# Channel attention: 12 of 49 tap tiles of exponentials summed by accumulating DMAs from GpSimd's queue, the total added by TensorE late in the tile

## The chip, the cores and the metric

The kernel runs on one core of one Trainium2 chip. The metric is the device time of one execution, in microseconds (us). PE is TensorE, DVE is VectorE, ACT is ScalarE, POOL is GpSimd, SP is SyncE.

## The reference, cut to what matters

Four layers run one after the other on an image tensor x of 4 x 256 x 64 x 64 float32: a windowed attention, a linear attention with grouped convolutions, a per-channel attention over 7 x 7 neighbours, and a dynamic 3 x 3 convolution. The change lies in the third alone:

```python
q = einsum('bchw,oc->bohw', x, w_q)
kmap = einsum('bchw,oc->bohw', x_pad, w_k)
vmap = einsum('bchw,oc->bohw', x_pad, w_v)
kwin = _unfold2d(kmap, 7)   # + rel_h on the first half of the channels, + rel_w on the other
attn = softmax(q[..., None] * kwin, axis=-1)     # over the 49 taps
out = sum(attn * vwin, axis=-1)
```

So each channel and pixel has 49 exponentials (taps), whose sum divides the sum of exponential times value.

## The kernel before, in words

`channel_attention` (from L1395) puts 128 channels on the partitions. A band is 16 image rows; 4 images make 16 bands (NB). A band has 4 tiles (TPB): 2 halves of the channels, and for each 2 tiles of 8 image rows, 512 pixels (TPX). In all that is 64 tiles of 49 taps. The taps of a tile are worked off in 7 rows of 7 taps ("row o" below is taps 7o to 7o+6). All engines have their order written out by hand: `all_bands(step)` calls a step for each tap of each tile on PE, ACT and DVE, and POOL loops over groups of 4 and 3 taps.

One step j does this:

- DVE (`multiply`, L1998) writes (key + relative bias) x query into one of 3 PSUM banks (`stage`, NST = 3). It waits until ACT has read the tap that used this bank before, so DVE is at most 3 taps ahead of ACT.
- PE (`step`, L1723) adds up the weighted values of tap j-12 (`sum_weighted`, V_LAG = 12), subtracts the upper bound from tap j (`shift`, L1679), and adds up the exponentials of tap j-2 (`sum_exponential`, E_LAG = 2). Both sums are 4 matmuls of 128x128 against an identity (`add_up`, L1686), which turn the tile and accumulate it in `pe_sum` or `pv_sum`.
- ACT (`exponential`, L1847) takes the exponential of tap j out of PSUM into a row buffer `se` (4 buffers of one row, NSE = 4). Before it writes into a buffer again it waits until PE has summed and POOL has weighted what was there. After tap 1 it copies the finished sum of the tile before into `es` (`take_e_sums`, L1835). After tap 46 it places the query of the next tile in PSUM (`place_query`, L1828).
- POOL (`weigh`, L1909) multiplies 4 or 3 taps of exponentials with the values into one of 4 buffers `ev`. PE reads them at step j+12.

Other work is placed at fixed steps. PE projects the next band's keys, queries and values (`project`, L1668): in the first tile of a half at steps 0, 7, 14, 24 and 29, in the second at 2, 6 and 12, each of two matmuls at two steps. DVE inverts the sum of the tile before in four pieces after steps 3, 5, 7 and 9 (`invert`, L2006), divides at step 12 (L2014), and makes the pairs and extremes of the next half's keys: `near_step_of` (L1946, L1950, L1958) at steps 11 to 30 of the first tile, after ACT's copy of the projection (L1821); `extreme_step` (L1974 to L1983) from step 34 of the first tile to step 46 of the second. ACT scales the next band at step 30 of the band's second tile (`normalise`, L1770).

Waits between the engines count on semaphores in units of taps, groups and tiles (`tiles(n, t, per, more)`).

Of the kernel before, what the change touches and what calls it, by code (L numbers as in the profile page):

```python
# [6 lines left out]
ACT = mybir.ActivationFunctionType  # L7
# [6 lines left out]
PART = 128  # L14
# [1368 lines left out]
K2 = 7  # L1383
# [11 lines left out]
def channel_attention(nc, sems, x_in, coef, x_out, stats, w_t, rel, ident_in, zeros):  # L1395
# [3 lines left out]
    with ctx:  # L1399
# [17 lines left out]
        top = [sb(f"top{u}", [PART, BPX], F32R) for u in range(2)]  # L1417
        se = [sb(f"se{i}", [PART, K2, TPX]) for i in range(NSE)]
        ev = [sb(f"ev{i}", [PART, ROW_PARTS[0][1], TPX]) for i in range(NEV)]
        es = sb("es", [PART, TPX])  # L1420
# [28 lines left out]
        exp_done = sem("exp_done")  # L1449
        weighted = sem("weighted")  # L1450
        e_summed = sem("e_summed")
        v_summed = sem("v_summed")
# [14 lines left out]
        ROWS_OF = {"0": (PAD, PAD), "1": (FRESH, RT), "2": (FRESH + RT, RT)}  # L1467
        E_LAG, V_LAG = 2, 12
        Q_AT = NTAP - NST
        INVERT_AT = (3, 5, 7, 9)  # L1470
# [20 lines left out]
        def tiles(n, t, per, more):  # L1491

            return n * (TPB * per) + (t * per + more)
# [65 lines left out]
        def before(t, j, lag):  # L1559

            back = t * NTAP + j - lag
            return back // NTAP, back % NTAP

        def bank_of(t, j):

            g = t * NTAP + j
            return 1 if g == TPB * NTAP - 1 else g % NST

        def bank_lag(t, j):

            return 2 if t * NTAP + j in (1, TPB * NTAP - 1) else NST

        def group_of(j):
            o, i = divmod(j, K2)
            return o * len(ROW_PARTS) + (i >= ROW_PARTS[1][0])
# [67 lines left out]
        def _(pe):  # L1643
# [38 lines left out]

            def add_up(acc, src, j):

                for c in range(NBLK2):
                    last = nc.tensor.matmul(acc[:, c * PART:(c + 1) * PART], lhsT=src[:, c * PART:(c + 1) * PART],  # L1686
                                            rhs=ident[:], is_transpose=True, start=j == 0 and c == 0,
                                            stop=j == NTAP - 1, skip_group_check=True)
                return last

            def sum_exponential(n, t, j, first=False):
                o, i = divmod(j, K2)
                if j == 0 and (t or not first):

                    pe.wait_ge(e_taken, tiles(n, t, 1, 0))
                pe.wait_ge(exp_done, tiles(n, t, NTAP, j + 1))
                add_up(pe_sum, se[(t * K2 + o) % NSE][:, i], j).then_inc(e_summed, 1)

            def sum_weighted(n, t, j, first=False):
                g = group_of(j)  # L1700
                i = j % K2 - ROW_PARTS[g % 2][0]
                if j == 0 and (t or not first):

                    pe.wait_ge(divided, tiles(n, t, 1, 0))
                if i == 0:
                    pe.wait_ge(weighted, tiles(n, t, NG2, g + 1))
                add_up(pv_sum, ev[(t * NG2 + g) % NEV][:, i], j).then_inc(v_summed, 1)

# [14 lines left out]
            def step(n, t, j, first=False, final=False):  # L1723
# [4 lines left out]
                shift(n, t, j)  # L1728
                if t * NTAP + j >= E_LAG or not first:
                    sum_exponential(n, *before(t, j, E_LAG), first=first)  # L1730
                if late:
                    sum_weighted(n, t, 0, first=first)
# [29 lines left out]
        def _(act):  # L1762
# [67 lines left out]
            def take_e_sums(n, t):  # L1830
                act.wait_ge(e_summed, tiles(n, t, NTAP, NTAP))
                if t > 0 or n:

                    act.wait_ge(inverted, tiles(n, t, NINV, 0))
                nc.scalar.activation(es[:], pe_sum[:], ACT.Copy).then_inc(e_taken, 1)  # L1835

            def exponential(n, t, j, first=False):
                o, i = divmod(j, K2)
                g = group_of(j)
                start, size = ROW_PARTS[g % 2]  # L1840
                if i == start and (t * NTAP + j >= NSE * K2 or not first):

                    t0, j0 = before(t, j, NSE * K2)
                    act.wait_ge(e_summed, tiles(n, t0, NTAP, j0 + size))
                    act.wait_ge(weighted, tiles(n, t0, NG2, group_of(j0) + 1))
                act.wait_ge(shifted, tiles(n, t, NTAP, j + 1))
                nc.scalar.activation(se[(t * K2 + o) % NSE][:, i], stage[:, bank_of(t, j), :], ACT.Exp)\  # L1847
                    .then_inc(exp_done, 1)

# [45 lines left out]
        def _(pool):  # L1895
            def weigh(n, t, g, first=False):
# [7 lines left out]
                if t * NG2 + g >= NEV or not first:  # L1904
# [4 lines left out]
                nc.gpsimd.tensor_tensor(split(ev[(t * NG2 + g) % NEV][:, 0:size]),  # L1909
                                        split(se[(t * K2 + o) % NSE][:, i:i + size]),  # L1910
                                        window(v[h], h, u, o, i, size), ALU.mult).then_inc(weighted, 1)

            for x in (xb, *k, *v, near, pair):
                nc.gpsimd.memset(x[:], 0.0).then_inc(cleared, 1)
            for n in range(NB):
                for t in range(TPB):
                    for g in range(NG2):
                        weigh(n, t, g, first=n == 0)

# [655 lines left out]
```

## Time and profile before

| what | us |
|---|---|
| three runs | 7983.3, 7987.79, 7996.58 |
| median | 7987.79 |
| the profiled execution's own time | 7993.27 |
| its span, first to last instruction | 7991.6 |
| channel attention, first to last multiply of DVE | 3314 to 7303 |

The profile is of one execution. Its own time is 5.5 us above the median of the runs. Matmuls are pipelined, and the profile models their ends: the mean of one says less than the distance from one start to the next. Where an engine's busy time fills a stretch, it had no wait there; what is missing is idle time. The two tiles whose rows are read below, called A and B, are the third and the fourth of one band: A (4940.74 to 5003.74 us) is the first tile of a half and has the near steps and the K and Q projections, B (5003.74 to 5063.33 us) is the second and has the V projections. A stretch runs from the start of DVE's multiply of tap 7o to that of tap 7o+7.

### The profile page before, as it was taken

Reading aid. Unit: us, or ns where it says so; the run is one execution under the profiler, and the core shown is the slowest. Engines: PE = TensorE matmul, PEld = TensorE weight load, DVE = VectorE, ACT = ScalarE, POOL = GpSimd, SP = SyncE. Lnnn points to the kernel's source line nnn. Section 1 sums busy time; section 2 is a strip of 40 time slices with the busy share of each in tenths; the row PEclk is TensorE's granted clock in tenths of the full one; section 3 lists DMA queues with packets and bytes.
Section 4 is the critical chain, followed back from the end, with each engine's and each line's share of the span. In section 5 each row is a group of like instructions: output and inputs, shape, how many; then the busy total and the mean of one; then the engine's idle time right before and its main releaser. Section 6 shows DMA issues by size and latency. Waiting matters only on the chain. (4 is left out here: it accounts for less than half of the span.)

```text
span 7991.6 us, 141890 instructions
## 1 busy us (share of the span) xinstructions
PE 7529.3 (94%) x55106; PEld 6489.6 (81%) x55106; DVE 5666.6 (71%) x8853; ACT 3670.7 (46%) x7040; POOL 4566.2 (57%) x2002
## 2 busy tenths in 40 slices
PE   5999998989998999599999999999999999997999
PEld 4777776879997776388888888888888888886999
DVE  5666665334443555688888888888888888896664
ACT  3655655423332332255555555555555555554222
POOL 3555552023332000388888888888888788886232
PEclk9999998999999999799999999999999999998999
DMA  3111113865557873100000000000000000002452
GB/s 142 61 58 67 60 58 122 282 161 144 144 147 194 234 210 109 29 20 23 27 18 17 20 23 27 18 18 19 24 27 18 17 20 24 27 9 93 138 164 78
DMA packets 633018, 617.21 MB, mean 77 GB/s; under 512 B 465525, under 2 KB 498421, under 8 KB 627174
## 3 DMA queue, kind: packets, MB, share of 16 engines
q1 hardware_dynamic: 581318, 483.44, 21.8%
q0 software_dynamic: 33856, 96.69, 3.3%
q10 hardware_dynamic: 17376, 30.54, 1.0%
q8 instruction: 330, 5.41, 0.3%
q14 instruction: 138, 1.13, 0.0%
HBM read 397.01 MB, written 193.76 MB: 74 GB/s over the span
## 5 line engine op out<-in xcount | busy, mean ns | idle before, releaser
L1909 POOL TENSOR_TENSOR e_ev<-e_se,e_v 128x2048 f32<-128x2048 f32 (+1 forms) x896 | 3307.7, 3712 | 760.6 <-ACT e_se L1847 758.1
L1847 ACT ACTIVATE e_se<-e_stage 128x512 f32<-128x512 f32 x3136 | 1867.8, 597 | 1851.4 <-PE e_stage L1679 1792.9
L1998 DVE SCALAR_TENSOR_TENSOR e_stage<-e_k,e_rl,e_qp 128x512 f32<-128x512 f32 x3136 | 2290.5, 747 | 340.7 <-ACT e_se L1847 285.7
L1686 PE MATMUL e_pe_sum<-e_ident,e_se 128*128 128x128 f32 x12544 | 1880.6, 272 | 16.5 <-ACT e_se L1847 12.3
L1686 PE MATMUL e_pv_sum<-e_ident,e_ev 128*128 128x128 f32 x12544 | 1875.4, 273 | 0.5 <-POOL e_ev L1909 0.5
L1686 PEld LDWEIGHTS e_pe_sum<-e_ident,e_se 128*128 128x128 f32 x12544 | 1550.6, 140 | 259.1 <-ACT e_es L1835 21.8
L1686 PEld LDWEIGHTS e_pv_sum<-e_ident,e_ev 128*128 128x128 f32 x12544 | 1477.2, 140 | 204.6 <-issue 203.2
L1679 PE MATMUL e_stage<-e_top,e_minus 128*128 128x512 f32 x3136 | 1507.8, 481 | 89.2 <-DVE e_stage L1998 85.6
L911 POOL DMA_DIRECT2D agg<-c_ot x384 | 334.6, 874 | 878.7 <-ACT c_ot L989 769.1
L403 POOL TENSOR_TENSOR a_pr<-a_pr,a_rden 128x480 f32<-128x480 f32 x512 | 494.1, 985 | 547.6 <-DVE a_rden L636 547.6
L1679 PEld LDWEIGHTS e_stage<-e_top,e_minus 128*128 128x128 f32 x3136 | 595.5, 190 | 143.6 <-DVE e_stage L1998 99.7
L596 ACT ACTIVATE a_pr<-a_ps,a_nmax 128x240 f32<-128x240 f32 x1024 | 459.3, 460 | 386.7 <-DVE a_nmax L630 386.7
L1974 DVE SCALAR_TENSOR_TENSOR e_ext<-e_near,e_rl,e_ext 128x512 f32<-128x512 f32 x768 | 575.3, 749 | 12.1 <-ACT e_ext L1857 11.4
L948 PE MATMUL c_pa<-c_x_high,c_w_high 128*128 128x448 f32 (+1 forms) x1440 | 522.6, 363 | 33.4 <-DVE c_w_low L1014 33.4
L948 PE MATMUL c_pa<-c_x_low,c_w_high 128*128 128x448 f32 (+1 forms) x1440 | 522.2, 363 | 0.0
L948 PE MATMUL c_pa<-c_x_high,c_w_low 128*128 128x448 f32 (+1 forms) x1440 | 522.0, 363 | 0.0
L630 DVE TENSOR_REDUCE a_nmax<-a_ps 128x2 f32<-128x480 f32 x512 | 312.9, 653 | 292.1 <-PE a_ps L484 285.0
L2294 PE MATMUL f_pc<-f_x_high,f_w_high 128*128 128x256 f32 x1536 | 440.3, 287 | 15.2 <-DVE f_xr L2474 13.0
L1958 DVE TENSOR_REDUCE e_near<-e_pair 128x192 f32<-128x768 f32 (+1 forms) x392 | 438.3, 1118 | 0.5
L2251 POOL TENSOR_TENSOR f_x_low<-f_xt,f_x_high 128x2560 fp32r<-128x2560 f32 x32 | 186.1, 5817 | 439.9 <-ACT f_x_high L2328 408.0
L2294 PE MATMUL f_pc<-f_x_low,f_w_high 128*128 128x256 f32 x1536 | 434.7, 283 | 0.0
L2294 PE MATMUL f_pc<-f_x_high,f_w_low 128*128 128x256 f32 x1536 | 434.1, 283 | 0.0
(175 smaller groups left out, 11567.5 us busy)
## 6 DMA issues: line engine op xcount, KB each, us to landing
qkv<-b_ot SPq DMA_DIRECT2D x120, 512.0 KB, 5.9
c_xt<-qkv SPq DMA_DIRECT2D x384, 160.0 KB, 3.8
agg<-c_ot POOLq DMA_DIRECT2D x384, 160.0 KB, 2.5
f_ws<-in_L_w_sets SPq DMA_DIRECT2D x32, 1152.0 KB, 7.9
a_xb<-in_x SPq DMA_DIRECT2D x24, 768.0 KB, 5.1
a_xr<-in_x SPq DMA_DIRECT2D x32, 512.0 KB, 3.8
x<-a_xr SPq DMA_DIRECT2D x32, 512.0 KB, 2.7
b_xc<-x SPq DMA_DIRECT2D x32, 512.0 KB, 5.8
```

The source lines that it names most:

```text
L403: nc.gpsimd.tensor_tensor(w, w, by, ALU.mult).then_inc(normalised, 1)
L596: last = nc.scalar.activation(pr[P % BUF][:, i, e, :], ps[:, 2 * s + i, e * NK:(e + 1) * NK], ACT.Exp, bias=nmax[P % BUF][:, i, e:e + 1], ...
L911: pool.dma_start(dst, ot[u][:, b]).then_inc(stored[u], 16)
L948: last = nc.tensor.matmul(pa[:, u, r, 0:(last_ - first) * WW].rearrange("p (k c) -> p k c", c=WW), lhsT=w[u][:, dx].rearrange("p o y -> p ...
L1679: nc.tensor.matmul(stage[:, bank_of(t, j), :], lhsT=minus[:], rhs=top[h][:, u * TPX:(u + 1) * TPX], start=False, stop=True, skip_group_che ...
L1686: last = nc.tensor.matmul(acc[:, c * PART:(c + 1) * PART], lhsT=src[:, c * PART:(c + 1) * PART], rhs=ident[:], is_transpose=True, start=j ...
L1847: nc.scalar.activation(se[(t * K2 + o) % NSE][:, i], stage[:, bank_of(t, j), :], ACT.Exp)\
L1909: nc.gpsimd.tensor_tensor(split(ev[(t * NG2 + g) % NEV][:, 0:size]), split(se[(t * K2 + o) % NSE][:, i:i + size]), window(v[h], h, u, o, i ...
L1958: nc.vector.tensor_reduce(grid(near[:, i])[:, first + low:first + low + part, PAD:PAD + WW], pairs, AX.XY, op)\
L1974: nc.vector.scalar_tensor_tensor(rows(ext[:]), win, r[:, o:o + 1], rows(ext[:]), ALU.add, op)\
L1998: nc.vector.scalar_tensor_tensor(rows(stage[:, bank_of(t, j), :]), win, rl[:, h, o:o + 1], rows(qp[:]), ALU.add, ALU.mult).then_inc(multip ...
L2294: last = nc.tensor.matmul(pc[:, m, s], lhsT=w[:, m, s * KW3 + dy, h], rhs=x[u][:, s, h, rows], start=dy == 0 and h == 0 and i == 0, stop=d ...
```

## The change

ACT writes the first 4 taps of row 0 into a new buffer `acc` (two of them, by tile parity, 4 x 512 elements on each partition) instead of `se`. At rows 1, 2 and 3, before POOL weighs the row's first group, POOL issues a DMA with accumulation that adds the row's first 4 taps in `se` onto `acc` (128 partitions x 8 KB, 1024 KB). The first of them waits for POOL's own weighting of `acc`, the others for the landing of the one before; each also waits for the exponentials that it reads. PE no longer sums the taps 0 to 3, 7 to 10, 14 to 17 and 21 to 24. It sums the other 33 as before, and the 4 tiles of `acc` at steps 42, 44, 46 and 48, after a wait for all three landings. `pe_sum` is opened by tap 4. ACT's waits for free buffers are recounted: for a buffer that was gathered it waits for the landing.

```diff
--- before.py
+++ after.py
@@ -1416,6 +1416,7 @@
         high = sb("high", [PART, BPX])
         top = [sb(f"top{u}", [PART, BPX], F32R) for u in range(2)]
         se = [sb(f"se{i}", [PART, K2, TPX]) for i in range(NSE)]
+        acc = [sb(f"acc{u}", [PART, ROW_PARTS[0][1], TPX]) for u in range(2)]
         ev = [sb(f"ev{i}", [PART, ROW_PARTS[0][1], TPX]) for i in range(NEV)]
         es = sb("es", [PART, TPX])
         rs = sb("rs", [PART, TPX])
@@ -1448,6 +1449,7 @@
         shifted = sem("shifted")
         exp_done = sem("exp_done")
         weighted = sem("weighted")
+        gathered = sem("gathered")
         e_summed = sem("e_summed")
         v_summed = sem("v_summed")
         e_taken = sem("e_taken")
@@ -1466,6 +1468,11 @@
         PROJ_AT = ({0: "K0", 7: "K1", 14: "K2", 24: "Q1", 29: "Q2"}, {2: "V0", 6: "V1", 12: "V2"})
         ROWS_OF = {"0": (PAD, PAD), "1": (FRESH, RT), "2": (FRESH + RT, RT)}
         E_LAG, V_LAG = 2, 12
+        GATHERED = (1, 2, 3)
+        NACC = ROW_PARTS[0][1]
+        DIRECT = [j for j in range(NTAP) if j % K2 >= NACC or j // K2 not in (0, *GATHERED)]
+        NES = len(DIRECT) + NACC
+        ACC_AT = (42, 44, 46, 48)
         Q_AT = NTAP - NST
         INVERT_AT = (3, 5, 7, 9)
         NINV = len(INVERT_AT)
@@ -1570,6 +1577,23 @@
 
             return 2 if t * NTAP + j in (1, TPB * NTAP - 1) else NST
 
+        def exps(t, j, taps=None):
+
+            o, i = divmod(j, K2)
+            buf = acc[t % 2] if o == 0 and i < NACC else se[(t * K2 + o) % NSE]
+            return buf[:, i] if taps is None else buf[:, i:i + taps]
+
+        def sums_made(n, t, j):
+
+            return tiles(n, t, NES, sum(d <= j for d in DIRECT) + sum(a < j + E_LAG for a in ACC_AT))
+
+        def gathers(n, t, o):
+
+            return 16 * tiles(n, t, len(GATHERED), sum(r <= o for r in GATHERED))
+
+        def part_of(j):
+            return group_of(j) % len(ROW_PARTS)
+
         def group_of(j):
             o, i = divmod(j, K2)
             return o * len(ROW_PARTS) + (i >= ROW_PARTS[1][0])
@@ -1680,21 +1704,26 @@
                                  rhs=top[h][:, u * TPX:(u + 1) * TPX], start=False, stop=True,
                                  skip_group_check=True).then_inc(shifted, 1)
 
-            def add_up(acc, src, j):
+            def add_up(total, src, opens_, closes):
 
                 for c in range(NBLK2):
-                    last = nc.tensor.matmul(acc[:, c * PART:(c + 1) * PART], lhsT=src[:, c * PART:(c + 1) * PART],
-                                            rhs=ident[:], is_transpose=True, start=j == 0 and c == 0,
-                                            stop=j == NTAP - 1, skip_group_check=True)
+                    last = nc.tensor.matmul(total[:, c * PART:(c + 1) * PART], lhsT=src[:, c * PART:(c + 1) * PART],
+                                            rhs=ident[:], is_transpose=True, start=opens_ and c == 0,
+                                            stop=closes, skip_group_check=True)
                 return last
 
             def sum_exponential(n, t, j, first=False):
-                o, i = divmod(j, K2)
-                if j == 0 and (t or not first):
+                if j == DIRECT[0] and (t or not first):
 
                     pe.wait_ge(e_taken, tiles(n, t, 1, 0))
                 pe.wait_ge(exp_done, tiles(n, t, NTAP, j + 1))
-                add_up(pe_sum, se[(t * K2 + o) % NSE][:, i], j).then_inc(e_summed, 1)
+                add_up(pe_sum, exps(t, j), j == DIRECT[0], j == DIRECT[-1]).then_inc(e_summed, 1)
+
+            def sum_gathered(n, t, i):
+
+                if i == 0:
+                    pe.wait_ge(gathered, gathers(n, t, K2))
+                add_up(pe_sum, acc[t % 2][:, i], False, False).then_inc(e_summed, 1)
 
             def sum_weighted(n, t, j, first=False):
                 g = group_of(j)
@@ -1704,7 +1733,7 @@
                     pe.wait_ge(divided, tiles(n, t, 1, 0))
                 if i == 0:
                     pe.wait_ge(weighted, tiles(n, t, NG2, g + 1))
-                add_up(pv_sum, ev[(t * NG2 + g) % NEV][:, i], j).then_inc(v_summed, 1)
+                add_up(pv_sum, ev[(t * NG2 + g) % NEV][:, i], j == 0, j == NTAP - 1).then_inc(v_summed, 1)
 
             def back(n, t, copies=0, near_=0):
 
@@ -1726,8 +1755,10 @@
                 if not late and (t * NTAP + j >= V_LAG or not first):
                     sum_weighted(n, *before(t, j, V_LAG), first=first)
                 shift(n, t, j)
-                if t * NTAP + j >= E_LAG or not first:
+                if (t * NTAP + j >= E_LAG or not first) and before(t, j, E_LAG)[1] in DIRECT:
                     sum_exponential(n, *before(t, j, E_LAG), first=first)
+                if j in ACC_AT:
+                    sum_gathered(n, t, ACC_AT.index(j))
                 if late:
                     sum_weighted(n, t, 0, first=first)
                 H = n * HALVES + t // 2 + 1
@@ -1828,7 +1859,7 @@
                 nc.scalar.activation(qp[:], q[h][:, u * TPX:(u + 1) * TPX], ACT.Copy).then_inc(query_placed, 1)
 
             def take_e_sums(n, t):
-                act.wait_ge(e_summed, tiles(n, t, NTAP, NTAP))
+                act.wait_ge(e_summed, tiles(n, t, NES, NES))
                 if t > 0 or n:
 
                     act.wait_ge(inverted, tiles(n, t, NINV, 0))
@@ -1838,14 +1869,23 @@
                 o, i = divmod(j, K2)
                 g = group_of(j)
                 start, size = ROW_PARTS[g % 2]
-                if i == start and (t * NTAP + j >= NSE * K2 or not first):
-
-                    t0, j0 = before(t, j, NSE * K2)
-                    act.wait_ge(e_summed, tiles(n, t0, NTAP, j0 + size))
-                    act.wait_ge(weighted, tiles(n, t0, NG2, group_of(j0) + 1))
+                if j == 0 and (t >= 2 or not first):
+
+                    act.wait_ge(e_summed, tiles(n, t - 2, NES, NES))
+                elif i == start and j:
+                    lag = NSE * K2
+                    if part_of(j) == 0 and before(t, j, lag)[1] == 0:
+                        lag *= 2
+                    if t * NTAP + j >= lag or not first:
+
+                        t0, j0 = before(t, j, lag)
+                        if part_of(j) == 0 and j0 // K2 in GATHERED:
+                            act.wait_ge(gathered, gathers(n, t0, j0 // K2))
+                        else:
+                            act.wait_ge(e_summed, sums_made(n, t0, j0 + size - 1))
+                        act.wait_ge(weighted, tiles(n, t0, NG2, group_of(j0) + 1))
                 act.wait_ge(shifted, tiles(n, t, NTAP, j + 1))
-                nc.scalar.activation(se[(t * K2 + o) % NSE][:, i], stage[:, bank_of(t, j), :], ACT.Exp)\
-                    .then_inc(exp_done, 1)
+                nc.scalar.activation(exps(t, j), stage[:, bank_of(t, j), :], ACT.Exp).then_inc(exp_done, 1)
 
             def open_extreme(H, s):
 
@@ -1907,14 +1947,26 @@
                     pool.wait_ge(v_summed, tiles(n, t0, NTAP, g0 // 2 * K2 + sum(ROW_PARTS[g0 % 2])))
                 split = lambda x: x.rearrange("p i (r c) -> p i r c", c=WW)
                 nc.gpsimd.tensor_tensor(split(ev[(t * NG2 + g) % NEV][:, 0:size]),
-                                        split(se[(t * K2 + o) % NSE][:, i:i + size]),
+                                        split(exps(t, o * K2 + i, size)),
                                         window(v[h], h, u, o, i, size), ALU.mult).then_inc(weighted, 1)
+
+            def gather(n, t, o):
+
+                if o == GATHERED[0]:
+                    pool.wait_ge(weighted, tiles(n, t, NG2, 1))
+                else:
+                    pool.wait_ge(gathered, gathers(n, t, o - 1))
+                pool.wait_ge(exp_done, tiles(n, t, NTAP, o * K2 + NACC))
+                flat = lambda x: x.rearrange("p i n -> p (i n)")
+                pool.dma_start(flat(acc[t % 2][:]), flat(se[(t * K2 + o) % NSE][:, 0:NACC]), accum_op=ALU.add).then_inc(gathered, 16)
 
             for x in (xb, *k, *v, near, pair):
                 nc.gpsimd.memset(x[:], 0.0).then_inc(cleared, 1)
             for n in range(NB):
                 for t in range(TPB):
                     for g in range(NG2):
+                        if g % 2 == 0 and g // 2 in GATHERED:
+                            gather(n, t, g // 2)
                         weigh(n, t, g, first=n == 0)
 
         @block.vector
```

## Rows read from the trace of the kernel before

**Rows 1.** The page: busy time of each engine
```profile
PE 7529.3 (94%) x55106; PEld 6489.6 (81%) x55106; DVE 5666.6 (71%) x8853; ACT 3670.7 (46%) x7040; POOL 4566.2 (57%) x2002
```
**Rows 2.** Stretches (us, busy time of each engine, clock, DMA): channel attention whole
```profile
core 0: us, PE busy (x) PEld busy (x) DVE busy (x) ACT busy (x) POOL busy (x), PEclk, DMA share, GB/s
3314.00:7303.00 3989.00, 3910.62 (x29214) 3410.48 (x29215) 3532.02 (x5089) 2129.41 (x3615) 3302.40 (x895) 1.00 0.07 20
```
**Rows 3.** Groups by line and shape, 4000 to 6000 us (busy, mean ns | idle before)
```profile
L1909 POOL TENSOR_TENSOR e_ev<-e_se,e_v 128x2048 f32<-128x2048 f32 x224 | 944.8, 4218 | 328.3 <-ACT e_se L1847 327.0 <-issue 1.3
L1686 PE MATMUL e_pe_sum<-e_ident,e_se 128*128 128x128 f32 x6260 | 938.5, 272 | 8.6 <-ACT e_se L1847 6.5
```
**Rows 4.** Stretches: rows 1, 2, 3, 6 of A, then 1, 2, 4, 6 of B
```profile
4948.44:4959.24 10.80, 10.64 (x77) 8.80 (x75) 8.31 (x15) 5.27 (x9) 8.69 (x3) 1.00 0.01 3
4959.24:4969.27 10.03, 10.03 (x73) 8.34 (x72) 10.03 (x17) 4.85 (x9) 7.49 (x3) 1.00 0.06 21
4969.27:4978.58 9.31, 9.17 (x63) 7.19 (x61) 9.31 (x16) 3.42 (x6) 7.75 (x3) 1.00 0.14 58
...
4995.68:5003.74 8.06, 8.06 (x67) 7.54 (x66) 7.28 (x13) 4.71 (x9) 7.73 (x3) 1.00 0.00 0
...
5012.29:5021.29 9.00, 9.00 (x64) 7.27 (x62) 8.83 (x14) 4.43 (x8) 6.67 (x3) 1.00 0.00 0
5021.29:5030.61 9.32, 9.32 (x68) 7.79 (x67) 7.00 (x12) 4.76 (x9) 7.23 (x3) 1.00 0.01 2
...
5038.85:5046.40 7.55, 7.55 (x64) 7.11 (x63) 6.74 (x11) 4.21 (x8) 7.22 (x3) 1.00 0.01 3
...
5054.76:5063.33 8.57, 8.57 (x72) 7.99 (x71) 6.65 (x12) 4.61 (x9) 8.23 (x3) 1.00 0.01 3
```
**Rows 5.** Timeline of PE, one plain step and one with a projection
```profile
4500.17 0.48 PE L1679 MATMUL e_stage<-e_top,e_minus 128*128 128x512 f32 x1
4500.49 0.60 PE L1686 MATMUL e_pe_sum<-e_ident,e_se 128*128 128x128 f32 x4
4500.92 0.60 PE L1686 MATMUL e_pv_sum<-e_ident,e_ev 128*128 128x128 f32 x4
4501.28 0.48 PE L1679 MATMUL e_stage<-e_top,e_minus 128*128 128x512 f32 x1
...
4514.68 1.04 PE L1668 MATMUL e_pj<-e_xb,e_wt 128*128 128x512 f32 x2
4515.56 0.60 PE L1686 MATMUL e_pv_sum<-e_ident,e_ev 128*128 128x128 f32 x4
```
**Rows 6.** Waits, 4000 to 6000 us (us in total, times, longest)
```profile
DVE e_rs L2006 <- ACT e_es L1835: 21.9, 32, 1.1
```
**Rows 7.** Timeline of DVE: two idle times in tile A, two in tile B
```profile
4944.89 0.95 DVE L2006 RECIPROCAL e_rs<-e_es 128x128 f32<-128x128 f32 x1 [0.76 <-ACT e_es L1835]
...
4955.97 0.17 DVE L1946 TENSOR_TENSOR e_pair<-e_pj,e_k 128x8 f32<-128x8 f32 x1 [1.90 <-ACT e_k L1821]
...
5026.05 0.75 DVE L1998 SCALAR_TENSOR_TENSOR e_stage<-e_k,e_rl,e_qp 128x512 f32<-128x512 f32 x1 [1.31 <-ACT e_se L1847]
...
5036.87 1.41 DVE L1998 SCALAR_TENSOR_TENSOR e_stage<-e_k,e_rl,e_qp 128x512 f32<-128x512 f32 x2
```
**Rows 8.** Timeline of GpSimd in tile B, from row 2
```profile
5029.33 7.38 POOL L1909 TENSOR_TENSOR e_ev<-e_se,e_v 128x2048 f32<-128x2048 f32 x2 [2.09 <-ACT e_se L1847]
```
**Rows 9.** DMA issues of the whole run (KB each, us to landing)
```profile
x<-d_xr POOLq DMA_DIRECT2D x32, 512.0 KB, 4.1
...
x<-e_xr SPq DMA_DIRECT2D x32, 512.0 KB, 2.7
...
e_near<-e_near ACTq DMA_DIRECT2D x12, 420.0 KB, 3.0
e_k<-e_k ACTq DMA_DIRECT2D x24, 210.0 KB, 2.2
```
**Rows 10.** The page: GpSimd's time for issuing one DMA
```profile
L911 POOL DMA_DIRECT2D agg<-c_ot x384 | 334.6, 874 | 878.7 <-ACT c_ot L989 769.1
```

## The prediction

> **What bounds the kernel now.** I read the page first, to see that no engine is full over the whole run and that PE comes nearest [rows 1]. The change touches channel attention alone, so the second view is the stretch of that stage: 3989 us of the 7992, PE busy 3911, DVE 3532, POOL 3302, at the full granted clock (1.00, so 2.4 GHz) [rows 2]. Per tile (64 of them) that is 62.3 us, of which DVE works 55.2 and POOL 51.6. PE looks like the bound, with DVE 7 us behind it. Over the stage that would promise much; but a tile is not even, so the third view cuts one pair of tiles into its rows of 7 taps [rows 4]. There the reader sees three kinds of row. In rows 2 and 3 of tile A, DVE is busy for the whole of 10.03 and 9.31 us: DVE sets the pace, whatever PE does. In row 6 of A PE is busy for all of 8.06 us and DVE for 7.28. In row 2 of B DVE works 7.00 of 9.32 us: PE sets the pace.
>
> What a step costs PE is read from starts in its timeline, not from the modelled mean of 272 ns a matmul [rows 3]: the shift starts at 4500.17, the sum of exponentials at 4500.49, the weighted sum at 4500.92 and the next shift at 4501.28. So four matmuls of the sum take 0.43 us, and a plain step 1.11, 7.75 a row. A projection's pair starts at 4514.68 and the next work at 4515.56: 0.88 more. All of these are in [rows 5].
>
> **The change part by part.**
> PE's sums: 12 fewer of 49, so 12 x 0.43 = 5.2 us a tile, 330 us over 64 tiles. That is the promise. But they are not removed evenly: 16 leave steps 2 to 26 (rows 0 to 3, four each, 1.74 us a row), and 4 come in at steps 42, 44, 46 and 48.
>
> The cost at the end: +4 x 0.43 = 1.74 us of PE in row 6, which is PE's own in both tiles (8.06 of 8.06 and 8.57 of 8.57 us [rows 4]). Can the start of the next tile take it back? PE must finish tap 48 at step 1 of the next tile; then ACT copies the sum, and DVE's first inversion waits for it: 32 times in 2000 us, 21.9 us in all, so 0.68 us at each tile's start [rows 6], one of them in front of 4944.89 [rows 7]. So that wait hangs on PE already, and the late sums move it by their whole length. From there DVE has no gap until row 1. Cost: 1.74 us a tile, 3.48 a pair, 111 us in all. A bound below: DVE might hide some of it in the idle time that row 6 of A has (8.06 - 7.28 = 0.78); at least 2.7 a pair remains.
>
> The gain in rows 0 to 3 is bounded by DVE's idle time there, since DVE is in order and its work does not change. Row 0 gives nothing: after the inversion starts DVE is full, and before it PE's old taps set the time. Row 1 of A: idle 10.80 - 8.31 = 2.49 us, of which 1.90 is the wait for ACT's copy of the projected keys [rows 7]. The copy comes after the exponential of step 9, and PE reaches that step earlier by the removed sum at 9 (0.43) and a part of those at 2 to 5: I take 0.8, between 0.4 and 1.7. Rows 2 and 3 of A: idle 0, gain 0. B: row 1 idle 0.17, row 2 2.32 [rows 4]. The large one in row 2 begins with 1.31 us [rows 7]: PE is late after the V projections at 12 and 13. With the sums of 9 to 12 and 16 to 19 gone, PE enters the projections caught up, and nearly all of it should go: 2.4. (That is 2.49 with row 1's, less 0.1.) Beyond it PE enters row 4 of B level with DVE; of its 0.81 idle I take 0.4. Gain: 0.8 + 2.4 + 0.4 = 3.6 us a pair, between 1.0 (the K1 wait and B's smaller gaps alone) and 5.8 (all the idle time named: 2.49 + 0.17 + 2.32 + 0.81).
>
> PE's wait for `e_taken` moves from step 2 to step 6; PE isn't the bound there: 0. ACT works 2129 of 3989 us [rows 2] and does the same exponentials; its new waits ask for landings some 28 taps (over 30 us) old: 0 unless the landings are very late. SP's queue is not passed by anything.
>
> POOL: 3 DMA issues more in a tile. The trace has POOL's time for one of 160 KB with 128 rows, 0.87 us [rows 10]; the issue here also has 128 rows. 3 x 0.87 = 2.6 us a tile; POOL then works 51.6 + 2.6 = 54.2 of 62. Behind each issue the row's weighing waits. Row 2 of B starts on POOL at 5029.33 and its first group takes 4.22 us [rows 8, 3], so ready at 5033.6; PE needs it at step 26, whose multiply is the second of the two that start at 5036.87 [rows 7], so about 4 us are to spare. Two issues (1.7 us) and a faster row (POOL's 7.4 + 0.9 = 8.3 us against some 7.6 for DVE) leave about 2. So 0, with 1 us a pair at worst.
>
> The landing of the DMA: nothing in the trace adds. Lower bound, a copy: 210 KB in SBUF lands in 2.2 us, 420 KB in 3.0, so 1024 KB in 3.0 + 604 x 0.8/210 = 5.3. The queue: 512 KB to memory lands in 4.1 from POOL and 2.7 from SP, 1.4 more, so 6.7 [rows 9]. Upper bound: if the destination's fetch doubles the part that grows with size (3.9), 10.6. I take 8.6, the middle of 6.7 and 10.6, since both rows are of plain copies. POOL comes to the next gather 8.3 us after the last at the earliest, so 8.6 costs 0.3, inside the 2 us to spare; 10.6 costs B some 2.5.
> The Trainium skill, Collectives: The Full Stack, section The bandwidth ceiling, says that a reduce is slower than a copy for its two source reads and not for the addition. With DMA: Bandwidth & Descriptors, Anatomy of one DMA (2.0 us and bytes over 436 GB/s), that makes an estimate of 2.0 + 2 x 2.4 = 6.8 us, and the sum would be the same with more to spare. No row here shows an addition.
>
> Sum: a pair loses 3.5 and gains 3.6; 32 pairs make -3 us. Against the profiled 7993.3 that is 7990; the profiled execution stands 5.5 above the median, so I forecast 7984. Its own range: from 7930 (gain 1.7 larger a pair) to 8040 (1.75 smaller).
>
> **The rivals.**
> 1. PE's relief arrives. For it: PE is busy 98% of the stage, and two idle times are waits behind PE's lag. Against: rows 2 and 3 of A. Price: the whole 5.8 us of idle time less 3.5 is 2.3 a pair, 74 us: 7914.
> 2. The landings are late (the other side). Gather 2 may not be issued before gather 1 has landed, and POOL's weighing stands behind it; then PE's weighted sums wait, in the shorter tile B first. It decides above about 10 us. Gather 3 is late by twice the excess over 8.3: at 12 us it is 7.4 less 2 to spare, 5.4 a pair, 173 us: 8160. At 15 us tile A joins and it is over 8400. For it: 10.6 is my upper bound for a mere double fetch. Against: the small landings of copies [rows 9].
> 3. The cost comes and the gain doesn't: the issues cost POOL more than 0.87 us or hold it in B's rows 1 to 3, where it has the least to spare, so that the freed PE waits for weighted values. Price: 3.5 - 1.0 = 2.5 a pair, 80 us: 8065.
> That the change does nothing is excluded by the code: 37 x 4 x 64 = 9472 matmuls remain of 49 x 4 x 64 = 12544.
>
> **How the numbers follow.** Forecast 0.42, rival 1 0.24, rival 2 0.18, rival 3 0.16. A measurement of this kernel tells 0.2% (16 us) from no change. The forecast's case lies 0.14 faster, 0.20 within and 0.08 slower; rival 1 is faster, the other two slower: 0.38, 0.20, 0.42. The range leaves out gains beyond the idle time that I named (0.08, below 7885, a further 0.9 a pair) and landings of about 12 us and more (0.12, above 8150): 7885 to 8150.
>
> **What would show it.** PE's sums of exponentials: 9472 matmuls. Row 6 of both tiles about 1.7 us longer, or the wait of DVE's inversion for `es` grown from 0.68 to 1.5 to 2.4 us. Rows 2 and 3 of A unchanged at 10.03 and 9.31. Row 2 of B down from 9.32 to about 7.2, with the 1.31 us idle time gone. Landings of 7 to 10 us, issues of 0.9. Wrong: a wait of PE for `e_ev`, or of POOL for a landing, of over 2 us a tile; or rows of B that stay as they are while PE is idle in them.

## The result: 33 us slower, and the profile after

The changed kernel takes 8027.39 us (median of 6 runs, 8020.29 to 8034.85) against 7994.59 for the kernel before, run beside it (6 runs, 7983.3 to 7999.68): ratio 1.0043, interval 1.003 to 1.0056. That is a small loss, twice what a measurement can tell from no change. The forecast had been 3 us faster.

The page first. This is its line of busy times, to be read beside [rows 1]:

```profile
PE 7347.2 (91%) x52034; PEld 6190.0 (77%) x52034; DVE 5652.9 (70%) x8853; ACT 3657.5 (46%) x7040; POOL 4728.6 (59%) x2194
```

PE has 3072 matmuls fewer, 12 x 4 x 64. Its busy time fell by 182 us; by the distance of its starts, 0.43 us for each of 768 sums, it has 330 us less to do (the ends behind the busy time are modelled). POOL has 192 instructions more. So the relief reached the engine, and the kernel is longer all the same: PE's busy time, 98% of the stage before, wasn't what alone bounded it. The groups by line and the DMA issues of the changed kernel show the new work itself (the issues: buffer, count, KB each, us to landing; the source line: its least, median and longest time from issue to landing):

```profile
L1710 PE MATMUL e_pe_sum<-e_ident,e_se 128*128 128x128 f32 x8448 | 1269.8, 273 | 5.4 <-ACT e_se L1888 5.4
e_acc<-e_se POOLq DMA_DIRECT2D x192, 1024.0 KB, 7.2
DMA to landing us min/median/max: 6.9/7.2/11.2
```

8448 matmuls from `se` and 1024 from `acc` make the 9472 predicted. The median landing takes 7.2 us. Now the same cut into rows as [rows 4], rows 0 to 3, 5 and 6 of a tile A, then rows 0 to 4 and 6 of the tile B behind it (us, busy time of PE, PEld, DVE, ACT, POOL, then granted clock, DMA share, GB/s):

```profile
4963.24:4972.01 8.77, 7.89 (x61) 6.83 (x59) 6.57 (x10) 5.26 (x9) 8.77 (x3) 1.00 0.07 25
4972.01:4982.34 10.33, 8.62 (x53) 6.47 (x54) 8.31 (x16) 4.46 (x8) 7.91 (x4) 1.00 0.13 26
4982.34:4992.31 9.97, 8.96 (x56) 6.62 (x55) 9.97 (x17) 4.73 (x9) 8.36 (x4) 1.00 0.59 129
4992.31:5001.61 9.30, 8.83 (x55) 6.51 (x53) 9.30 (x15) 4.22 (x8) 8.50 (x4) 1.00 0.74 178
5010.28:5018.21 7.93, 7.93 (x66) 7.37 (x65) 6.87 (x10) 4.77 (x8) 7.57 (x3) 1.00 0.09 35
5018.21:5027.15 8.94, 8.94 (x76) 8.49 (x75) 7.38 (x13) 4.68 (x8) 7.73 (x3) 1.00 0.01 2
5027.15:5036.57 9.42, 8.16 (x61) 6.86 (x59) 7.88 (x11) 5.78 (x10) 8.58 (x3) 1.00 0.00 0
5036.57:5045.30 8.73, 7.96 (x48) 5.86 (x49) 8.73 (x14) 4.65 (x8) 5.66 (x4) 1.00 0.01 2
5045.30:5054.30 9.00, 8.87 (x60) 6.97 (x59) 6.91 (x12) 4.93 (x10) 7.99 (x4) 1.00 0.58 117
5054.30:5062.14 7.84, 7.08 (x53) 6.02 (x52) 7.84 (x14) 4.19 (x7) 7.44 (x3) 1.00 0.67 136
5062.14:5068.98 6.84, 6.84 (x54) 6.01 (x53) 6.55 (x12) 3.62 (x7) 6.06 (x3) 1.00 0.75 153
5077.33:5086.78 9.45, 9.45 (x82) 8.94 (x80) 6.75 (x12) 4.61 (x9) 9.45 (x4) 1.00 0.00 1
```

Read against [rows 4]: rows 2 and 3 of A lost their PE work (10.03 to 8.96 and 9.31 to 8.83) and none of their length (9.97 and 9.30), because DVE is busy for all of both. Row 6 grew from 8.06 to 8.94 in A and from 8.57 to 9.45 in B, with PE busy throughout. Row 2 of B, where the forecast had its largest gain, went from 9.32 only to 9.00. One pair can be a chance one, so here are means over tiles 8 to 55, worked out from the starts of DVE's multiplies in the two timelines (us from tap 7o to tap 7o + 7, before to after):

| row | tile A | tile B |
|---|---|---|
| 0 | 8.06 to 8.86 | 8.55 to 9.43 |
| 1 | 10.66 to 10.36 | 9.13 to 8.73 |
| 2 | 11.23 to 11.27 | 9.32 to 8.99 |
| 3 | 10.22 to 10.23 | 8.24 to 7.84 |
| 4 | 9.26 to 8.98 | 8.47 to 7.75 |
| 5 | 7.93 to 7.93 | 8.26 to 8.38 |
| 6 | 8.05 to 8.93 | 7.89 to 8.75 |

Rows 0 and 6 of both tiles lose 0.80 + 0.88 + 0.88 + 0.86 = 3.42 us a pair. The other rows win about 2.25 net. The difference, some 1.15 us a pair, is 37 us over 32 pairs, close to the 33 measured; nearly all of it falls on tile A (+1.15), while B comes out level (+0.02). The late sums of a tile lengthen the next tile's row 0 too; if that row is charged to the tile whose sums they are, A stands at +1.23 and B at -0.07, which says the same.

The 0.12 in row 5 of B comes from one row in one tile, the 38th. A gather there landed after 11.0 us, and POOL, which waits for it, had been idle for 4.41 us when it went on 1.7 us later (what held it for these 1.7 is not shown). PE then stood idle for 2.64 us until POOL had weighed, and after that the granted clock fell from 2.4 to 1.2 GHz for some steps. First the row in the changed kernel (clock 0.84, 11.00 us), then the same row in the kernel before, then PE's lines:

```profile
5704.71:5715.71 11.00, 10.48 (x72) 9.73 (x73) 8.29 (x13) 4.72 (x9) 11.00 (x5) 0.84 0.18 33
5677.23:5685.40 8.17, 8.17 (x69) 7.67 (x67) 8.00 (x14) 4.96 (x9) 8.17 (x3) 1.00 0.01 1
```
```profile
5705.23 0.66 PE L1710 MATMUL e_pv_sum<-e_ident,e_ev 128*128 128x128 f32 x4 [2.64 <-POOL e_ev L1949]
5706.45 1.06 PE L1710 MATMUL e_pv_sum<-e_ident,e_ev 128*128 128x128 f32 x4
5707.16 0.77 PE L1703 MATMUL e_stage<-e_top,e_minus 128*128 128x512 f32 x1
```

From 5706.45 to 5707.16 the four matmuls take 0.71 us; at the full clock the same ones take 0.35. The trace has ten such short stretches at 1.2 GHz inside channel attention, where the kernel before has two. Set beside the same rows of other tiles, the rows in which they fall are longer by an estimated 6 us in sum, against 3 before: a small part of the 33.

Next the waits from 4000 to 6000 us (engine, what it produces, line, what it waited for, us in total, times, longest); the first is that of [rows 6]:

```profile
DVE e_rs L2058 <- ACT e_es L1866: 26.3, 32, 1.1
PEld e_stage L1703 <- DVE e_stage L2050: 215.7, 329, 2.8
DVE e_pair L1998 <- ACT e_k L1852: 11.4, 6, 1.9
POOL e_acc L1961 <- DMA e_acc<-e_se: 8.4, 5, 2.3
PEld e_pv_sum L1710 <- POOL e_ev L1949: 5.1, 5, 2.9
PE e_stage L1703 <- DVE e_stage L2050: 133.4, 255, 2.6
```

POOL waited for a landing 5 times in these 2000 us, 8.4 us in all, and PE for POOL's weighted values 5.1 us: neither is where the time went. The second and the last line are the ones to look at, PE's wait for DVE's multiplies as its weight loads see it and as its matmuls see it. In the kernel before they were

```profile
PEld e_stage L1679 <- DVE e_stage L1998: 49.7, 88, 2.5
PE e_stage L1679 <- DVE e_stage L1998: 27.9, 56, 2.2
```

The weight loads wait 215.7 - 49.7 = 166 us longer for DVE's multiplies, 5.2 us for each of the 32 tiles in these 2000 us; the matmuls wait 105.5 us longer, 3.3 a tile. The profile counts each from its own last end, and the matmuls' ends are modelled. A tile has 12 sums fewer in all, 12 x 0.43 = 5.2 us of PE's work, and did not get shorter, so PE must stand idle for at least that much longer: these waits say that most of it goes into waiting for DVE.

### The profile page after: what moved, and what is told of

Same layout as the page of the kernel before. It is cut to its first block and busy times, and to the rows that moved or that the text cites. A ratio compares the mean times of both kernels' runs of the same rounds, so it can differ in the third digit from the quotient of the medians.

```text
span 8033.2 us, 136128 instructions
## 1 busy us (share of the span) xinstructions
PE 7347.2 (91%) x52034; PEld 6190.0 (77%) x52034; DVE 5652.9 (70%) x8853; ACT 3657.5 (46%) x7040; POOL 4728.6 (59%) x2194
## 5 line engine op out<-in xcount | busy, mean ns | idle before, releaser
L1949 POOL TENSOR_TENSOR e_ev<-e_se,e_v 128x1536 f32<-128x1536 f32 (+1 forms) x832 | 3095.5, 3906 | 143.5 <-ACT e_se L1888 142.8
L1888 ACT ACTIVATE e_se<-e_stage 128x512 f32<-128x512 f32 x2880 | 1707.7, 598 | 1789.6 <-PE e_stage L1703 1758.5
L1703 PE MATMUL e_stage<-e_top,e_minus 128*128 128x512 f32 x3136 | 1528.0, 487 | 302.5 <-DVE e_stage L2050 293.6
L1710 PEld LDWEIGHTS e_pv_sum<-e_ident,e_ev 128*128 128x128 f32 x12544 | 1502.8, 141 | 308.1 <-issue 204.8
L1710 PE MATMUL e_pe_sum<-e_ident,e_se 128*128 128x128 f32 x8448 | 1269.8, 273 | 5.4 <-ACT e_se L1888 5.4
L1710 PEld LDWEIGHTS e_pe_sum<-e_ident,e_se 128*128 128x128 f32 x8448 | 1052.2, 140 | 161.9 <-ACT e_se L1888 8.5
```

Of the source, the lines that this page charges most:

```text
L1703: nc.tensor.matmul(stage[:, bank_of(t, j), :], lhsT=minus[:], rhs=top[h][:, u * TPX:(u + 1) * TPX], start=False, stop=True, skip_group_che ...
L1710: last = nc.tensor.matmul(total[:, c * PART:(c + 1) * PART], lhsT=src[:, c * PART:(c + 1) * PART], rhs=ident[:], is_transpose=True, start= ...
L1888: nc.scalar.activation(exps(t, j), stage[:, bank_of(t, j), :], ACT.Exp).then_inc(exp_done, 1)
```

## The experiments

The kernel before ran beside each, and its median stayed between 7994.5 and 7996.8. Where a run is compared with the changed kernel, the 8027.39 from above is meant, which was not measured again beside it; such differences can be off by a few us. In the expectations "theory 1" is that the late sums cost what they add and that the relief reaches few of the waits; its rivals stand with each.

### Without the late sums

```
-        NES = len(DIRECT) + NACC
-        ACC_AT = (42, 44, 46, 48)
+        NES = len(DIRECT)
+        ACC_AT = ()
```

> The changed kernel without PE's four late sums of the gathered tiles; the DMAs and the removed sums stay. Left out: 16 of the 49 exponentials never reach the total. Theory 1 (the four late sums cost what rows 0 and 6 of both tiles grew by, 3.4 us a pair of tiles, 110 us in all): 8027 falls to about 7918, some 77 us faster than the kernel before. Theory 2 (the time is lost to GpSimd's issues or to the traffic of the accumulating DMAs, which stay): about 8027, no change from the changed kernel.

Measured: 7924.6 us (4 runs, 7920.81 to 7929.66), ratio to before 0.9911 [0.9896, 0.9926], as theory 1 had it. Its total lacks the 16 gathered taps, so this is a probe and no version to use. The stretches of this kernel, columns as above: row 6 of A, row 0 of B, then row 6 of B:

```profile
4969.10:4977.15 8.05, 8.05 (x67) 7.55 (x66) 7.27 (x12) 4.72 (x9) 7.69 (x3) 1.00 0.01 2
4977.15:4985.70 8.55, 7.27 (x54) 6.07 (x52) 7.70 (x12) 5.68 (x10) 8.55 (x3) 1.00 0.00 0
5026.45:5035.01 8.56, 8.56 (x72) 7.98 (x71) 6.65 (x11) 4.61 (x9) 8.56 (x3) 1.00 0.01 3
```

Both rows 6 are back at the 8.06 and 8.57 of before. So the late sums cost 8027.4 - 7924.6 = 103 us, 3.2 a pair (forecast 3.48, 111 us), and all the relief together is worth 7996.8 - 7924.6 = 72 us, 2.25 a pair (forecast 3.6, 115 us). The error is in the gain.

### The DMAs alone

The kernel before, with the 192 accumulating DMAs, their waits on POOL and ACT's waits for the landings, but into buffers that nothing reads; PE makes all 49 sums.

```
+                        if g % 2 == 0 and g // 2 in GATHERED:
+                            gather(n, t, g // 2)
```

> The kernel before, with PE summing all 49 tiles itself, plus the 192 accumulating DMAs from GpSimd into a buffer that nobody reads, and ACT's waits for their landing. Theory 1: within 10 us of the kernel before, about 7995. Theory 2: slower than the kernel before by 30 us or more, 8025 and up.

Measured: 7998.45 us (10 runs), ratio 1.0004 [0.9995, 1.0014]. The transfers are the same as in the changed kernel:

```profile
e_acc<-e_se POOLq DMA_DIRECT2D x192, 1024.0 KB, 7.2
```

Issues, POOL's waits and the traffic cost nothing that can be told. In this run PE is not relieved, so alone it does not exclude rival 3, by which a relieved PE waits for POOL. The changed kernel's own waits do: PE waited for `e_ev` 5.1 us in 32 tiles. Late landings, rival 2, show in the tile above, whose row 5 was 2.8 us longer; as the cause of the loss both rivals fall.

### The total taken earlier

Only rows 1 and 2 are gathered, and PE adds the total at steps 27 to 30, where the trace showed PE waiting for DVE.

```
-        GATHERED = (1, 2, 3)
+        GATHERED = (1, 2)
-        ACC_AT = (42, 44, 46, 48)
+        ACC_AT = (27, 28, 29, 30)
```

> The changed kernel with rows 1 and 2 gathered alone (8 sums fewer instead of 12), and PE's sums of the gathered tiles at steps 27 to 30, where the changed kernel's PE waits for DVE (lag 0.05 us), instead of 42 to 48. Theory 1: the 3.4 us a pair go, of row 3's gain some 0.5 is given back: 90 us below the changed kernel, about 7935, faster than both. Theory 2: only a third of the DMA cost goes, about 8015.

Measured: 8023.33 us (6 runs), ratio 1.0032 [1.002, 1.0045]. The expectation failed: almost nothing was won, and that is no proof of theory 2 (about 8015) either, since the run with the DMAs alone has shown that they cost nothing. Row 4 of A and row 4 of B in this kernel:

```profile
4993.05:5003.96 10.91, 10.91 (x84) 9.37 (x82) 7.21 (x11) 5.17 (x9) 5.33 (x3) 1.00 0.18 49
5054.05:5062.54 8.49, 8.49 (x73) 8.05 (x72) 6.76 (x12) 3.63 (x7) 8.09 (x3) 1.00 0.01 3
```

Rows 0 and 6 did return to their old lengths, but row 4 took the cost over: 10.91 us where the changed kernel has 8.67 in A, and 8.49 against 6.84 in B. In means over tiles 8 to 55 it is 10.51 against 8.98 and 9.66 against 7.75, 3.44 us a pair, as much as rows 0 and 6 gave back. PE's idle time had been that of one step, 27. Over steps 27 to 30 of tile A DVE takes 6.28 us and PE, with two projections, 4 x 1.11 + 2 x 0.88 = 6.2: level, so four sums more are 1.7 us more. In tile B PE was busy for all of row 4 (6.84 of 6.84 us). An engine that waits at one step has no slack in the row. The run changes two things, the place of the total and row 3's four sums, which PE makes itself again; how much of row 4's growth is theirs was not separated. As they stand, this place is no better than the one at the end.

### Where the relief went in tile B: the third V projection

DVE's and PE's timelines of the changed kernel, taps 16 to 19 and PE's steps 12 to 14 ahead of them (start, us, engine, line; in brackets the idle time before and what ended it):

```profile
5047.87 0.75 DVE L2050 SCALAR_TENSOR_TENSOR e_stage<-e_k,e_rl,e_qp 128x512 f32<-128x512 f32 x1
5049.73 0.75 DVE L2050 SCALAR_TENSOR_TENSOR e_stage<-e_k,e_rl,e_qp 128x512 f32<-128x512 f32 x1 [1.11 <-ACT e_se L1888]
5050.76 0.75 DVE L2050 SCALAR_TENSOR_TENSOR e_stage<-e_k,e_rl,e_qp 128x512 f32<-128x512 f32 x1 [0.28 <-ACT e_se L1888]
5051.87 0.75 DVE L2050 SCALAR_TENSOR_TENSOR e_stage<-e_k,e_rl,e_qp 128x512 f32<-128x512 f32 x1 [0.35 <-ACT e_se L1888]
```
```profile
5044.19 0.50 PE L1703 MATMUL e_stage<-e_top,e_minus 128*128 128x512 f32 x1 [0.53 <-DVE e_stage L2050]
5044.79 0.66 PE L1710 MATMUL e_pv_sum<-e_ident,e_ev 128*128 128x128 f32 x4
5045.28 1.04 PE L1692 MATMUL e_pj<-e_xb,e_wt 128*128 128x512 f32 x2
5046.16 0.60 PE L1710 MATMUL e_pv_sum<-e_ident,e_ev 128*128 128x128 f32 x4
5046.51 0.48 PE L1703 MATMUL e_stage<-e_top,e_minus 128*128 128x512 f32 x1
5046.83 0.60 PE L1710 MATMUL e_pe_sum<-e_ident,e_se 128*128 128x128 f32 x4
5047.27 1.04 PE L1692 MATMUL e_pj<-e_xb,e_wt 128*128 128x512 f32 x2
5048.15 0.60 PE L1710 MATMUL e_pv_sum<-e_ident,e_ev 128*128 128x128 f32 x4
```

The 1.31 us of [rows 7] became 1.11, and the gaps behind it are still there. At step 12 PE is level with DVE and cannot be more: its shift waits 0.53 us for DVE's multiply of that tap (5044.19), and its first weighted sum (5044.79) then waits for DVE's division of the tile before, 13.0 us in 32 tiles:

```profile
PEld e_pv_sum L1710 <- DVE e_od L2066: 13.0, 32, 0.4
```

Then come two projections of 0.88, and between and behind them the sums of taps 11 to 13, which are not gathered. The removed sums of row 2 would have stood at steps 16 to 19: behind the place that makes DVE wait. If that is the cause, the projection moved behind them should win:

```
-  PROJ_AT = (..., {2: "V0", 6: "V1", 12: "V2"})
+  PROJ_AT = (..., {2: "V0", 6: "V1", 16: "V2"})
```

> The changed kernel with the second V projection of a half moved from steps 12 and 13 to steps 16 and 17, away from the steps where PE waits for DVE's division and where the sums of taps 11 to 13 were kept. Theory 1 (DVE's idle time of 1.1 us in front of tap 17's multiply in tile B and 0.27 to 0.35 at the next three hangs on that): 1.0 to 2.0 us a pair go, 8027 falls to 7963 to 7995. Rival (the projections' 1.76 us only move, and PE is as late four steps later): within 10 us of 8027.

Measured: 8005.86 us (10 runs), ratio 1.0009 [1.0, 1.0019], 21 us below the changed kernel. The direction is theory 1's and the size is missed: 0.7 us a pair, where 1.0 to 2.0 were expected. Rows 2 and 3 of B:

```profile
5023.95:5031.93 7.98, 7.98 (x56) 6.43 (x55) 6.80 (x11) 4.23 (x9) 7.98 (x4) 1.00 0.65 131
5031.93:5040.10 8.17, 7.58 (x58) 6.53 (x57) 7.94 (x13) 5.03 (x9) 8.17 (x4) 1.00 0.65 130
```

Row 2 falls from 9.00 to 7.98 and row 3 gives back 0.33 (7.84 to 8.17). The same move in the kernel before tells whether the place alone does it:

> The kernel before with the last V projection at step 16 instead of 12, nothing else. Theory 1 (there PE is busy for the whole of rows 1 to 3 of tile B, so the move only shifts its lag): within 10 us of the kernel before. Rival (the place of that projection is bad by itself): 20 us or more faster.

Measured: 7997.92 us (10 runs), ratio 0.9999 [0.999, 1.0009]: nothing. The move wins only where the sums are gone, so what it lets through is the relief.

### Where it went in tile A: the key projection

In rows 0 and 1 of tile A the relief reaches PE and little of it goes further: DVE works without a gap from its first inversion to tap 10, and PE waits for its multiplies, as here at step 4:

```profile
4970.06 0.50 PE L1703 MATMUL e_stage<-e_top,e_minus 128*128 128x512 f32 x1 [0.53 <-DVE e_stage L2050]
```

DVE's wait for ACT's copy of the second keys in the changed kernel still is what it was in [rows 7]:

```profile
4979.07 0.17 DVE L1998 TENSOR_TENSOR e_pair<-e_pj,e_k 128x8 f32<-128x8 f32 x1 [1.90 <-ACT e_k L1852]
```

Two causes were possible: an inversion of DVE's in the way, or the copy's own place, behind PE's projections at steps 7 and 8. The first, in the kernel before:

```
-        INVERT_AT = (3, 5, 7, 9)
+        INVERT_AT = (3, 5, 7, 11)
```

> The kernel before with DVE's fourth inversion after step 11 instead of 9, so that in tile A it lies in DVE's wait of 1.7 to 1.9 us for ACT's copy of the projected keys. Theory 1 (that wait is DVE's real idle time and row 1 of A is held by DVE's order, not by PE's sums): 0.7 to 0.9 us a pair, 22 to 29 us faster than the kernel before. Rival (PE's sums hold row 1): no change.

Measured: 7998.89 us (11 runs), ratio 1.0003 [0.9994, 1.0012]: the expected gain of over 20 us did not come. DVE in this kernel:

```profile
4958.25 0.76 DVE L1998 SCALAR_TENSOR_TENSOR e_stage<-e_k,e_rl,e_qp 128x512 f32<-128x512 f32 x1 [1.15 <-ACT e_se L1847]
...
4960.90 0.17 DVE L1946 TENSOR_TENSOR e_pair<-e_pj,e_k 128x8 f32<-128x8 f32 x1 [1.04 <-ACT e_k L1821]
```

The idle time was divided in two, 1.15 and 1.04, and not shortened. The copy comes when PE and ACT bring it. So the second cause, in the changed kernel:

```
-  PROJ_AT = ({0: "K0", 7: "K1", ...}, ...)
+  PROJ_AT = ({0: "K0", 6: "K1", ...}, ...)
```

> The changed kernel with the K1 projection of a half at steps 6 and 7 instead of 7 and 8, so that ACT copies the keys after the exponential of tap 8 instead of 9. Theory 1 (in row 1 of tile A the relief does not reach DVE because DVE waits 1.66 us for that copy, behind the two projections): the copy comes a PE step of 0.67 us or more earlier, 0.6 to 1.1 us a pair, 20 to 35 us below 8027, about 8000. Rival (PE's sums set row 1 anyway): 8027.

Measured: 8000.14 us (10 runs), ratio 1.0003 [0.9994, 1.0012], 27 us below the changed kernel. Row 1 of A and DVE's line in it:

```profile
4950.91:4960.13 9.22, 8.63 (x53) 6.46 (x54) 8.21 (x15) 4.68 (x8) 7.19 (x4) 1.00 0.08 17
```
```profile
4956.87 0.17 DVE L1998 TENSOR_TENSOR e_pair<-e_pj,e_k 128x8 f32<-128x8 f32 x1
```

The row falls from 10.33 to 9.22 (10.36 to 9.44 in the mean) and the wait for the copy is gone; 1.01 us of idle time before the multiply of tap 11 remains. And in the kernel before:

> The kernel before with K1 at step 6 alone: the control. Theory 1: 0.3 to 1.1 us a pair, 10 to 35 us faster than the kernel before. Rival: no change, and then a gain in the changed kernel is the removed sums' own.

Measured: 7978.44 us (8 runs), ratio 0.9976 [0.9966, 0.9986], 18 us faster, and row 1 of A falls from 10.66 to 10.05 in the mean. Of the move's 27 us, 18 thus have nothing to do with the sums. With K1 at step 6 in both kernels the relief shortens row 1 of A by 0.61 (10.05 to 9.44) and not by 0.30: the other half was hidden behind the copy.

### The change in tiles B only

Tiles A add all 49 sums on PE, tiles B as in the change. The counts of the semaphores are rewritten to suit; the core is

```
+        def direct_of(t):
+            return DIRECT if t % 2 else list(range(NTAP))
-                if j in ACC_AT:
+                if j in ACC_AT and t % 2:
-                        if g % 2 == 0 and g // 2 in GATHERED:
+                        if t % 2 and g % 2 == 0 and g // 2 in GATHERED:
```

> The changed kernel with the gathers in the second tile of a half (B) alone; the first (A), where DVE sets the pace in rows 2 and 3, sums all 49 itself. Theory 1 (late sums cost 0.86 us at each of two places a tile, and A's relief gives back only 0.3 in row 1 and 0.3 in row 4): 1.7 less cost and 0.6 less gain a pair, 35 to 40 us below the changed kernel, about 7990, the kernel before within 0.2%. Rival (the relief in A is worth what it costs): no change from 8027.

Measured: 7989.07 us (11 runs), ratio 0.9991 [0.9982, 1.0]. As expected, the loss is gone, and as the table of means said: it lay in A. With V2 at step 16 too:

> The same with the last V projection at step 16 instead of 12. Theory 1: the 0.76 us a pair that the move gave in the changed kernel comes on top, another 24 us, about 7966, some 30 us faster than the kernel before. Rival (the move helped only because tile A gathered too): about 7990.

Measured: 7971.58 us (6 runs), ratio 0.9968 [0.9956, 0.998]: 17 us of the 24 expected. With K1 at step 6 besides:

> Gathers in the second tiles alone, V2 at step 16, K1 at step 6. Theory 1: the copy comes up to a step earlier here too, but PE is full in row 1 of A (all sums kept), so 0.3 to 1.1 us a pair: 7972 falls to 7937 to 7962, faster than all before. Rival: 7972.

Measured: 7956.96 us (5 runs), ratio 0.9948 [0.9935, 0.9962], the fastest version here that makes the whole computation, and faster than both kernels. Last, both moves with the gathers in both tiles:

> The changed kernel (gathers in all tiles) with both moved projections, V2 at step 16 and K1 at step 6. Theory 1, every part read so far adds up: 8027 less 21 (V2) less 27 (K1) is 7979, some 18 us faster than the kernel before but 22 us behind the version that gathers in the second tiles alone: tile A's gather still costs more than it gives. Rival (with the projections out of the way A's relief comes through in full): at or below 7957.

Measured: 7974.85 us (6 runs), ratio 0.9969 [0.9957, 0.9981]. That is the 7979 expected, within 5 us, and 18 us behind the version with gathers in B alone; the intervals overlap a little, so that the gathers of tile A still cost more than they give is likely and not beyond doubt.

## Why the prediction was wrong

The cost was read rightly in size; the gain was mis-sized, above all in row 2 of B, and with a net of two nearly equal terms that turned the sign. Step by step:

- **PE's 12 sums fewer, 330 us of promise.** 3072 matmuls are gone. That DVE would not let most of it through was right: rows 2 and 3 of A kept their length (11.23 to 11.27, 10.22 to 10.23).
- **The late sums, 3.48 us a pair.** Right in size: 3.42 by the rows, 3.2 by the run without them. The place was half wrong. The prediction had row 6 longer by 1.7 or DVE's wait for `es` grown to 1.5 or more; the wait is 26.3 / 32 = 0.82 (0.68 before), and each tile pays 0.87 in row 6 and about as much in the next row 0. DVE's multiplies need banks that PE's shifts and ACT's exponentials must free, so DVE is held along the way and not once at the end (four waits for ACT in row 0 of the changed tile A, 2.2 us in all, against two of 1.2 in the kernel before).
- **Row 1 of A, 0.8 taken.** It gave 0.30. The failed step is "PE reaches that step earlier by the removed sum at 9 (0.43) and a part of those at 2 to 5". PE is not earlier by the sums of steps 2 to 5, since DVE is full there and PE waits for its multiplies (0.53 us at step 4, 0.49 at step 6); the time won is lost at the next multiply. The copy's own place, behind two projections, decides: moving it won 27 us and 18 us.
- **Row 2 of B, 2.4 taken for rows 1 and 2.** They gave 0.40 + 0.33 = 0.73. This is the largest error, 1.7 us a pair or 53 us, more than the whole miss. The failed step is "PE enters the projections caught up, and nearly all of it should go". PE does enter them caught up, and the idle time stays (1.11 of 1.31): level with DVE is the most that PE can be, since its shift waits for DVE's multiply and its first weighted sum for DVE's division; then two projections and three ungathered sums put it behind again, and of the removed sums that the prediction counted here, those of steps 16 to 19 come only after them. Moving V2 behind these steps won 21 us with the change and nothing without it. That is less than half of the 53, and the rest stays open. What the two waits at step 12 cost is read from the trace; no run removed them.
- **Row 4 of B, 0.4 taken.** It gave 0.72, and row 3 another 0.40 and row 4 of A 0.28, of which the prediction counted none: part of the relief arrives a row later than I looked for it. The terms that I had named gave 0.30 + 0.73 + 0.72 = 1.75; these two, less 0.17 lost in other rows (0.12 of it the one row with the late landing), make it 2.26.
- **DMA issues, 0.** Right: the run with the DMAs alone is 1.0004. An issue took 0.87 us in the median (mean 0.90, longest 1.49), against a mean of 0.874 in [rows 10].
- **The landing, 8.6 us within 5.3 to 10.6.** The median is 7.2 us, so a gather has mostly landed before POOL comes to the next one; the trace puts 13 of POOL's waits down to it, 24.6 us in all, and the longest landing took 11.2, above the 10.6 named as the upper bound. By the Trainium skill (Collectives: The Full Stack, The bandwidth ceiling, with DMA: Bandwidth & Descriptors, Anatomy of one DMA) the estimate had been 6.8; the trace agrees within 0.4 us of the median, though no run shows the second read by itself; the sum would not have changed.
- **The rivals.** Rival 1 (7914) would have needed all of DVE's idle time; of its 5.8 us a pair the relief took 2.25. Rivals 2 and 3 end on the right side for reasons that are not there, or are there in one tile of 64. (Rival 3's 80 us make 8068 from the 7988 that rival 1 starts from, and not 8065; nothing hangs on it.) What happened is the lower half of the forecast's own case, whose range of 7930 to 8040 holds 8027: gain 2.25 a pair instead of 3.6. The chance of slower within that case, 0.08 of 0.42, was too small for a term known only between 1.0 and 5.8 against a fixed cost of 3.5.

## What to carry to other kernels

In this kernel, work taken off one engine was worth only what it shortened of another engine's wait. Where the relieved engine met a partner that was itself full, or a wait for that partner's result, the time won was gone. So list for each removed instruction the next wait behind it, and count no gain beyond that wait. Work added where an engine sets the pace cost nearly its whole length (3.2 to 3.4 us of 3.5), and a wait at one step was no slack where the engine was busy over the rest of the row. When a relief lands behind the place that is late, try moving that place: here a projection moved by four steps and another by one won 52 us together in the changed kernel (8027 to 7975), more than the 33 that the change had lost.

## What the runs showed of the hardware

Landing times: an accumulating transfer of 1024 KB within SBUF landed in 7.2 us (median; least 6.9, longest 11.2, 8 of 192 above 10), 1.4 times the 5.3 that I estimated for a plain copy of that size from [rows 9]. The DMA share of row 3 of A rose from 0.14 to 0.74, and the run with the DMAs alone, at the same transfers, lost no measurable time. POOL's records of weighing changed form beside the issues: from 4000 to 6000 us the mean of a group of 128x2048 is 4455 ns and not 4218 [rows 3]:

```profile
L1949 POOL TENSOR_TENSOR e_ev<-e_se,e_v 128x2048 f32<-128x2048 f32 x190 | 846.4, 4455 | 70.9 <-ACT e_se L1888 70.8
L1949 POOL TENSOR_TENSOR e_ev<-e_acc,e_v 128x2048 f32<-128x2048 f32 x32 | 135.6, 4237 | 22.3 <-ACT e_acc L1888 22.3
```

The second line is row 0's group, which has no issue ahead of it and kept its length. But an issue directly ahead is not the condition: in means over tiles 8 to 55 the groups of rows 4 to 6 of tile B, with no issue among them, are 4.50 to 4.60 us long too (4.22 before), while those of rows 4 to 6 of tile A stayed at 4.21 to 4.23. Where POOL has no wait between the two groups of a row, the second starts 4.15 to 4.2 us behind the first in both kernels, so a longer record was not a longer row; what the record holds more was not tried.
